# Graph kernel: the sums of two attention layers get more buffers, an earlier load, and a residual that partly moves to TensorE

## The reference, cut to what matters

```python
def gat_conv(x, src, dst, W, a_src, a_dst, b, num_nodes):
    h = jnp.einsum('nd,dhf->nhf', x, W)
    logits = jax.nn.leaky_relu(al_s[src] + al_d[dst], 0.2)
    e = jnp.exp(logits - m[dst])                    # softmax over the edges of a target node
    alpha = e / (z[dst] + 1e-16)
    out = jax.ops.segment_sum(h[src] * alpha[..., None], dst, num_segments=num_nodes)
    return out + b
h   = gat_conv(x, ..., W1, ...)                     # 8 heads
out = gat_conv(h, ..., W2, ...)                     # 1 head
x   = _layernorm(x + out)
```

## Time and profile before

| what | value |
|---|---|
| median of 3 runs | 3779.49 us (3779.07 to 3781.46) |
| the profiled execution's own time | 3806.31 us |
| span of its trace | 3804.5 us |
| busy in the span | PE 3222.5, PEld 2659.1, DVE 2782.3, ACT 1886.4, POOL 2084.1 us |
| softmax of layer 1, by the trace | about 506 to 571.9 us |
| `gat1` | 571.9 to 731.3 us |
| `gather_out1` | 731.3 to 1035.8 us |
| `gat2` | 1035.8 to 1285.45 us |

### The profile page before, as it was taken

One profiled execution on the slowest core, in us unless ns is written; L12 is line 12 of the kernel. 1 busy time (PEld: TensorE's weight loads), 2 busy tenths in 40 slices (PEclk: granted clock), 3 DMA queues, 4 the chain that ended last, 5 costly groups with the idle time before them and its releaser, 6 DMA issues. The chain is left out here.

```text
span 3804.5 us, 56930 instructions
## 1 busy us (share of the span) xinstructions
PE 3222.5 (85%) x15070; PEld 2659.1 (70%) x15070; DVE 2782.3 (73%) x7844; ACT 1886.4 (50%) x5403; POOL 2084.1 (55%) x2118
## 2 busy tenths in 40 slices
PE   5999935588577599856999996999999999999775
PEld 4888824476466366534888885888888787878664
DVE  5666667699688366675677665989989898989742
ACT  3777724466433112134333332666666566666565
POOL 3666600267267566424333333767677676767577
PEclk8999967799799899978999998999999999999997
DMA  4877839644267332247343333878878686868664
GB/s 139 242 242 238 242 106 302 225 128 133 67 197 219 96 89 88 59 145 234 95 125 121 120 119 117 242 210 235 240 212 251 194 252 198 252 200 248 198 218 162
DMA packets 677043, 684.78 MB, mean 180 GB/s; under 512 B 72882, under 2 KB 631015, under 8 KB 676627
## 3 DMA queue, kind: packets, MB, share of 16 engines
q1 hardware_dynamic: 592122, 484.38, 40.8%
q0 software_dynamic: 68160, 181.21, 17.5%
q10 hardware_dynamic: 16444, 15.55, 1.2%
HBM read 401.66 MB, written 283.11 MB: 180 GB/s over the span
## 5 line engine op out<-in xcount | busy, mean ns | idle before, releaser
L2823 PE MATMUL s_i_bank<-s_i_messages,s_i_equal 128*128 128x256 f32 x1200 | 360.5, 383 | 6.9 <-issue 4.4
L622 POOL DMA_INDIRECT s_i_messages<-h,table_row x300 | 305.6, 1019 | 98.0 <-issue 80.8
L932 POOL TENSOR_TENSOR n_powers<-n_powers,neg_half 128x8 f32<-128x8 f32 (+3 forms) x164 | 268.0, 1634 | 165.6 <-issue 59.3
L622 POOL DMA_INDIRECT s_i_messages<-h,table_row_b x300 | 309.2, 1031 | 90.1 <-issue 81.8
L857 ACT ACTIVATE n_z<-gamma_bc,n_powers 128x256 f32<-128x256 f32 x320 | 175.0, 594 | 354.9 <-POOL n_powers L932 354.0
L816 PE MATMUL s_n_bank<-w,n_xt 128*128 128x256 f32 x1280 | 309.1, 385 | 17.8 <-DMA n_xt<-in_x_t 16.8
L834 PE MATMUL s_n_bank<-w_out,n_ht 128*128 128x256 f32 x1280 | 314.0, 390 | 6.5 <-ACT n_ht L844 6.3
L825 PE MATMUL s_n_bank<-n_x3t,w_in 128*128 128x256 f32 x1280 | 303.3, 380 | 0.0
L2852 DVE SCALAR_TENSOR_TENSOR s_i_y<-s_i_bank,s_i_scale,acc 128x256 f32<-128x256 f32 x600 | 285.6, 477 | 5.0 <-remote 5.0
L816 PEld LDWEIGHTS s_n_bank<-w,n_xt 128*128 128x128 f32 x1280 | 246.9, 193 | 53.7 <-DMA n_xt<-in_x_t 17.2
L834 PEld LDWEIGHTS s_n_bank<-w_out,n_ht 128*128 128x128 f32 x1280 | 248.5, 195 | 46.5 <-ACT n_ht L844 11.7
(11 more groups left out here) (452 smaller groups left out, 9268.8 us busy)
## 6 DMA issues: line engine op xcount, KB each, us to landing
h<-s_i_y SPq DMA_DIRECT2D x600, 128.0 KB
n_xt<-in_x_t SPq DMA_DIRECT2D x160, 256.0 KB
out<-n_w SPq DMA_DIRECT2D x160, 256.0 KB
s_i_equal<-eq_tab SPq DMA_DIRECT2D x600, 64.0 KB
x<-s_x_rows SPq DMA_DIRECT2D x100, 256.0 KB
out<-s_a_hs SPq DMA_DIRECT2D x100, 128.0 KB
proj_dst<-s_a_hd SPq DMA_DIRECT2D x100, 128.0 KB
h<-s_h_rows SPq DMA_DIRECT2D x50, 256.0 KB
```

The costliest lines, as they stand in the source:

```text
L622: return net.nc.gpsimd.indirect_dma_start(out, None, table, bass.IndirectOffsetOnAxis(index, 0))
L932: self.nc.gpsimd.tensor_tensor(v[:, 8 + b0:8 + b1], v[:, b0:b1], self.net.neg_half[:, 0:b1 - b0], ALU.pow).then_inc(self.powered, 1)
L2823: nc.tensor.matmul(banks[r % 4][:, 0:D], EQ[q % NM][:], M[q % NM][:], start=True, stop=True).then_inc(summed, 1)
```

## The change

Three places are rewritten.

1. `softmax` of layer 1 now also loads the first seven units of `gat1`: SP issues them behind the load of `src_nodes`. Their buffers (`Feed`, tiles `b_equal` and `b_x`) are allocated around both stages.
2. `gat1` has seven buffers for its loads; unit k's table and features are loaded when unit k - 7 is summed. The keys of the search are the first thing that SP loads in the stage.
3. `gat2` has five buffers for the table and `out1`, six for the gathered `x`, four for `y`, and four PSUM banks for the projection. PE does `total(i)` first in a turn, DVE weighs a unit earlier, POOL issues the gathers ahead of the power. For the first tile of each unit the residual is added by PE: a product of the gathered rows with `spread` (an identity whose row 0 is ones; row 0 of the gathered tile holds the constant `c12`, its gather being sent out of bounds) starts the accumulation. DVE then adds the residual of the second tile alone and takes the first tile's statistics from PSUM, and ACT normalises it from there.

```diff
@@ softmax, SyncE
                 sp.dma_start(net.src_nodes[:], ...).then_inc(nodes_in, 16)
+                for k in range(feed.NB):
+                    feed.load(sp, k)
                 sp.wait_ge(nodes_in, 16)
@@ class Feed: NB = 7
+    def load(self, sp, k):
+        net, b, R = self.net, k % self.NB, self.net.R
...
+        sp.dma_start(self.EQ[b][:], net.eq_tab[tiles, :, :]...).then_inc(self.eq_in[b], 16)
+        sp.dma_start(self.X[b][:, :, 0, :], net.out1[rows, :]...).then_inc(self.x_in[b], 16)
+        sp.dma_start(self.X[b][:, :, 1, :], net.proj_dst[tiles, :, :]...).then_inc(self.x_in[b], 16)
@@ gat1, SyncE
-            for k in range(2):
-                load(k)
             find.load(sp)
-            for k in range(2, N):
-                load(k)
+            for k in range(NB, N):
+                sp.wait_ge(summed, k - NB + 1)
+                sp.wait_ge(msg_ready, k - NB + 1)
+                feed.load(sp, k)
@@ gat2
-    G, NB = 2, 3
+    G, NB, NE, NX = 2, 5, 5, 6
-        Y = st.sb("d_y", [P, G, D], n=3)
+        Y = st.sb("d_y", [P, G, D], n=4)
-        sums, tps, prs = (st.ps(f"d_ps_{n}", 2) for n in ("sums", "t", "p"))
+        sums, tps, prs = (st.ps(f"d_ps_{n}", m) for n, m in (("sums", 2), ("t", 2), ("p", 4)))
@@ gat2, SyncE
-                load(i + 2)
+                load(i + 3)
@@ gat2, GpSimd
+            gp.wait_ge(based, NX + 4)
...
+                get(i + 2)
                 power(i - 3)
-                get(i + 2)
@@ gat2, TensorE, project(k)
                     pe.wait_ge(xt_ready, k + 1)
-                    past(pe, y_ready, k - 1)
+                    pe.wait_ge(x_in[k % NX], ...)
+                    past(pe, x1_ready, k - 3)
                     for g in range(w):
+                        if k < N and g == 0:
+                            nc.tensor.matmul(out, spread[:], X[k % NX][:, g, :], start=True, stop=False)
...
             for i in range(TURNS):
+                total(i)
                 transposes(i - 1)
                 project(i - 2)
-                total(i)
@@ gat2, ScalarE, norm(k)
+                        y = prs[k % 4][0:p, 0:D] if g == 0 else Y[k % 4][:, 1, :]
@@ gat2, VectorE
+            def stats(k):
...
+                    if k < N:
+                        V.tensor_tensor(Y[k % 4][:, 1, :], prs[k % 4][:, D:2 * D], X[k % NX][:, 1, :], ALU.add)
+                    ch(V.bn_stats(s[0:p, 0:6], prs[k % 4][0:p, 0:D]))
+                    if k < N:
+                        ch(V.bn_stats(s[:, 6:12], Y[k % 4][:, 1, :]))
+            for b in range(NX):
+                V.tensor_copy(X[b][0:1, 0, :], net.c12[0:1, :]).then_inc(based, 1)
...
+            weigh(0)
             for i in range(TURNS):
-                weigh(i)
+                weigh(i + 1)
                 aggregate(i - 1)
                 bias(i - 2)
-                join(i - 3)
+                stats(i - 3)
```

More of the change, by code:

```diff
@@ L1274, in _, with softmax @@
                     src.var_1(dve, *v)
-def softmax(net, layer):
+def softmax(net, layer, feed=None):
     nc, T, H = net.nc, net.T, net.H
@@ L1512, in count, with __init__, gat1 @@
             ct.then_inc(self.counted, 1)
-def gat1(net):
+class Feed:
+    NB = 7
+    def __init__(self, net, ctx):
+        nc, self.net, self.G = net.nc, net, 2
+        sb = lambda name, shape: [ctx.enter_context(nc.sbuf_tensor(f"{name}{i}", shape, F32)) for i in range(self.NB)]
+        self.EQ = sb("b_equal", [P, self.G, P])
+        self.X = sb("b_x", [P, self.G, 2, net.D])
+        self.eq_in = [nc.alloc_semaphore(f"b_eq_loaded{i}") for i in range(self.NB)]
+        self.x_in = [nc.alloc_semaphore(f"b_x_loaded{i}") for i in range(self.NB)]
+    def load(self, sp, k):
+        net, b, R = self.net, k % self.NB, self.net.R
+        tiles = slice(k * self.G, (k + 1) * self.G)
+        rows = slice(R + k * self.G * P, R + (k + 1) * self.G * P)
+        sp.dma_start(self.EQ[b][:], net.eq_tab[tiles, :, :].rearrange("g p e -> p g e")).then_inc(self.eq_in[b], 16)
+        sp.dma_start(self.X[b][:, :, 0, :], net.out1[rows, :].rearrange("(g p) d -> p g d", p=P)).then_inc(self.x_in[b], 16)
+        sp.dma_start(self.X[b][:, :, 1, :], net.proj_dst[tiles, :, :].rearrange("g p d -> p g d")).then_inc(self.x_in[b], 16)
+def gat1(net, feed):
     nc, D, T, R, H = net.nc, net.D, net.T, net.R, net.H
-    G, NB = 2, 4
+    G, NB = feed.G, feed.NB
     N = T // G
     with Stage(nc) as st:
-        EQ = st.sb("b_equal", [P, G, P], n=NB)
-        X = st.sb("b_x", [P, G, 2, D], n=NB)
+        EQ, X, eq_in, x_in = feed.EQ, feed.X, feed.eq_in, feed.x_in
         M = st.sb("b_messages", [P, G, 2, D], n=2)
@@ L1531, in gat1 @@
         find = Search(net, st)
-        eq_in, x_in = (st.sem(f"b_{n}", NB) for n in ("eq_loaded", "x_loaded"))
         ends_out, stored = (st.sem(f"b_{n}", m) for n, m in (("ends_stored", 3), ("out1_stored", 3)))
@@ L1892, in store @@
                     sp.wait_ge(x1_ready, k + 1)
-                    sp.dma_start(tiles(net.x1, k), Y[k % 3][:]).then_inc(stored[k % 3], 16)
-            for k in range(2):
+                    sp.dma_start(tiles(net.x1, k), Y[k % 4][:]).then_inc(stored[k % 4], 16)
+            for k in range(3):
                 load(k)
             for i in range(TURNS):
-                load(i + 2)
+                load(i + 3)
                 store_ends(i - 1)
@@ L1908, in get @@
                 if k <= N:
-                    past(gp, y_ready, k - NB + 1)
+                    past(gp, y_ready, k - NX + 1)
                 if k < N:
@@ L1951, in total @@
                         for g in range(G):
-                            mm = nc.tensor.matmul(sums[k % 2][:, g * D:(g + 1) * D], EQ[k % NB][:, g, :], net.out1_src[:, k * G + g, :], start=True, stop=True)
+                            mm = nc.tensor.matmul(sums[k % 2][:, g * D:(g + 1) * D], EQ[k % NE][:, g, :], net.out1_src[:, k * G + g, :], start=True, stop=True)
                         mm.then_inc(summed, 1)
@@ L3010, in build @@
                 project1(net)
-                with nc.sbuf_tensor("src_nodes", [net.T, net.R], I32) as net.src_nodes:
-                    softmax(net, 1)
-                    gat1(net)
+                with nc.sbuf_tensor("src_nodes", [net.T, net.R], I32) as net.src_nodes, ExitStack() as feed_ctx:
+                    feed = Feed(net, feed_ctx)
+                    softmax(net, 1, feed)
+                    gat1(net, feed)
             with nc.sbuf_tensor("scores_2", [P, 2, net.T], F32) as net.scores, nc.sbuf_tensor("out1_src", [P, net.T, net.D], F32) as net.out1_src:
```

82 lines of the change are left out of this document (43 added, 39 removed).

## The result

The changed kernel took 3756.17 us in the median of four runs (3753.27 to 3758.17), the kernel before 3780.47 on the same chip: a ratio of 0.9927 (95% interval 0.9914 to 0.994), 24.3 us or 0.7% faster. The sign was right and the stated range of 3726 to 3757 us held the time, but by 0.8 us, and with luck: the likeliest case's own range ended at 3751, and the rest was there for a rival (late loads) that did not come. The gain is 16 us short of the 40.3 that were forecast. The profiled execution after took 3758.17 us by its own time, with a span of 3756.5.

A forecast was written before the change was run, and what follows sets the result against it. The first sums were taken as bound by transfers, the second sums by a ring of waits with a 4.21 us lap. Terms 4.8 + 5.5 + 30.0 + 0 = 40.3 us off the median 3779.49 gave 3739 us, range 3726 to 3757.

The forecast's parts named there:

- the likeliest case: Whole kernel: all terms together gain 40.3 us, to 3739 us, own range 3730 to 3751; chance 64%.
- late loads: Second sums: a store waiting for lagging POOL holds the next table; turn 3.85, gain 27.9 us, 3752; chance 10%.
- Load in the softmax: Softmax: 4.59 MB of added transfers hide under its work, cost 0; without that cover, 13 us.
- Start of the first sums: Start of gat1: keys issued first land earlier, so everything up to turn 1 starts 4.8 us earlier (3.7 to 5.7).
- Turns of the first sums: gat1 after turn 1: three units' less data left for the DMA-bound stretch, gain 5.5 us (3.5 to 7.5).
- Turns of the second sums: gat2 steady part: 46 turns fall from 4.233 to 3.58 us, gain 30.0 us (25.0 to 32.8).
- The ring: gat2 before the change: aggregate, transposes, projection and sums wait on each other in turn, one lap 4.21 us.
- GpSimd locked out: gat2: gathers wait for DVE's weighing pass (0.47 us), turn about 4.1, gain 16.4 us, 3763; chance 8%.
- The ring stays: gat2: some wait keeps the turn at 4.21; gain 5.9 us, 3774, no change; chance 3%.
- slower: gat2: PE falls from 2.4 to 1.2 GHz, turn 7.04 us; with 20 such turns 3808 us; chance 3%.
- Ramp and tail: Start and end of gat2: aggregates come 3.2 us earlier, the tail gives back 3.3; together 0 (-4 to +3).
- The base: Whole kernel: the 40.3 us are taken off the median before, 3779.49, rather than the profiled 3806.31, giving 3739.

The follow-up runs named there:

- the second trace: The unchanged kernel before, run and traced once more: 3783.42 us, span 3781.6.
- experiment 3: Changed kernel with its seven buffers, but all their loads issued in the first sums' own stage, none in the softmax: ratio 0.9942 to the kernel before.
- the first trace: The kernel before, in the profiled execution that the prediction was made from: 3806.31 us by its own time, span 3804.5.
- Experiments 4: Changed kernel with both gathers of a unit of the second sums without an index bound: ratio 0.987 to the kernel before.
- experiment 6: Changed kernel with bounded gathers kept and the shift product moved from GpSimd to VectorE: ratio 0.9867 to the kernel before.
- experiment 10: Changed kernel with both gathers plain and ScalarE writing the constant into row 0 afterwards: ratio 0.9859 to the kernel before.
- experiment 5: Changed kernel with the x1 stores of the second sums issued from ScalarE's queue: ratio 0.9919 to the kernel before.
- experiment 9: Changed kernel with plain gathers in the second sums, the residual of both tiles on VectorE and no product with spread: ratio 0.9893 to the kernel before.
- experiment 8: Kernel before with an index bound on both gathers of the second sums, all indices inside the table: 3787.12 us in a single run.

## Why the prediction was right, and where not

**Load in the softmax, 0:** right. The softmax took 65.6 us (65.4 and 65.5 before); its DMA share is 0.84 from 540 to 550 us and 0.00 from there to 565, so the loads had ended 15 us ahead of the border.

**Start of the first sums, 4.8:** 4.9 by the second trace (18.0 to 13.1), 5.3 by experiment 3.

**Turns of the first sums, 5.5:** 124.1 to 117.7 is 6.4 us, 5.7 by the first trace (123.4 to the same pass). It is less data left behind turn 1, as forecast: over these 123.4 and 117.7 us both kernels move 341 GB/s, so 1.9 MB less, for the 1.97 MB of three units. The rate didn't rise. The rule with 425 GB/s of the Trainium skill, page "DMA: Bandwidth & Descriptors", section "Where 436 GB/s comes from", would have given 17.6 us; no run here shows that rate.

**Turns of the second sums, 30.0:** the step that failed. It measured 17.0 (46 turns from 4.265 to 3.895; 15.6 by the first trace). The ring is gone, TensorE's turn was 3.46 for a forecast 3.52, VectorE was under it. But "POOL's turn ... 3.69 us" was put together from the gathers of before, and the diff's gathers carry a bound that those don't: the lap is 3.95. The surplus over TensorE is then 0.45 to 0.5 us a turn, some 20 us over the stage, where I let buffers of "about three turns or 10 us" absorb 8. They were used up after a few turns, and from there the turn is GpSimd's. Experiments 4, 6 and 10 show it from three sides, each with a turn of 3.45. My 3.69 was too high as well: for plain gathers it counts a gap of 0.30 behind the product, which is 0.16 in experiment 10, and 0.28 for the product, which is 0.20 there; the lap is 3.46. With them my term would have been 46 x (4.265 - 3.45) = 37 us.

**Rivals.** *Late loads* gave nearly the measured turn and time (3.85 and 3752), for a wrong cause. The sign that I had named for it even came, a turn over 3.8 and VectorE waiting for a table (3.5 us in 120), so that sign could not tell the two apart; experiment 5 did, where the waits for tables were gone and the turn stayed at 3.855. *GpSimd locked out* had a price of that size too (0.47 us a turn); against it, VectorE is busy 108.0 of 120 us in experiment 10, 95.7 in the changed kernel, and the gathers take 0.99 us in the mean there, 1.08 and 1.00 here. So the lock of the Trainium skill, page "SBUF — State Buffer", section "SBUF: two separate sides", is not what lengthened them. A hold of this kind does show, on another instruction: the product of experiment 9, and the 0.28 us product of the earlier trace rows, which ends 0.05 us behind the bias pass in 29 turns of the second trace of before. In the changed kernel the product stands clear of the bias pass and takes 0.20. *The ring stays* and *slower* didn't come; the clock is 1.00 in the steady part. Of the signs of the likeliest case, the turn of 3.5 to 3.7 us and the aggregates without a wait didn't come either.

**Ramp and tail, 0:** held. The fourth aggregate came 15.5 us after the stage's start, where the first trace of before had 19.7 and the second 17.1: 4.2 or 1.6 us gained for a forecast 3.2. From the last aggregate to the next stage it takes 40.0 us, for 35.2 and 36.0: 4.7 or 3.9 lost for 3.3. Together -0.6 or -2.4 us, inside -4 to +3. The sizes agree in part by luck: the sums of unit N started 9.6 us behind that aggregate, where it was 8.1 and 7.9, a term that the forecast had at nothing, and the work behind them took 3.2 or 2.2 us more. The products that queue there, after:

```profile
1219.44 1.15 PE L1970 MATMUL s_d_ps_sums<-s_d_ends,upper 100*100 100x256 f32 x2 [8.50 <-DMA s_d_ends<-ends]
...
1222.08 3.26 PE L2001 MATMUL s_d_ps_p<-w,s_d_xt 128*128 128x256 f32 x8
```

Four products took 3.26 us here, 0.8 each, against 0.47 in mid-stage. The window of 1222.0 to 1225.5 has a mean granted clock of 0.59, and the one ahead of it 0.50, TensorE's lower level of 1.2 GHz, behind 8.50 us in which it stood idle:

```profile
1218.00:1222.00 4.00, 2.56 (x8) 2.16 (x9) 0.76 (x2) 0.53 (x2) 0.00 (x0) 0.50 0.10 39
1222.00:1225.50 3.50, 3.50 (x12) 2.78 (x11) 0.12 (x1) 1.01 (x3) 0.00 (x0) 0.59 0.24 80
```

**The base** was sound: taking the gain from the median and not from the first trace's 3806 kept its 26 us of scatter out.

**Left open:** what GpSimd does in the 0.77 us between a bounded gather's MOVE and its start (experiment 8). That they can overlap earlier work is seen in experiment 6; what they consist of, nothing here shows.

## What to carry to other kernels

When a change gives an instruction one more argument, its price is not that of the instruction in the old trace: ask what the argument adds to the lap of the engine that will be the fullest, and whether buffers really cover the surplus times the number of turns. Behind a change with several parts, look for the engine that waits for nobody; the waits of the others (ends, tables, aggregates) were its consequences. Name signs that tell two rivals apart: a wait for tables belonged to both here. And try the buffers alone before moving work to an engine: here they gave 28.6 us, while the moved residual cost 14.0 until its bound was taken away, and was then worth 9.3.

## What the runs showed of the hardware

A gather with a bound on its indices took 1.00 to 1.08 us where a plain one took 0.95 to 1.02, but it also started 0.5 us later after the wait that let it go (0.80 for 0.28 us), and 0.54 instead of 0.16 us behind a GpSimd product of 0.20; behind the power of 0.81 the gap was 0.19, and behind another gather 0.30 either way. The bounded first gather of a unit starts 0.77 us behind a MOVE of GpSimd that plain gathers don't have (33 of 33 turns of the changed kernel). A GpSimd product of 128x2 that started inside VectorE's bias pass ended 0.05 us behind that pass (39 of 39 turns of experiment 9); gathers that started inside it were not held (6 in experiment 6, 1.06 to 1.10 us). Nor was VectorE held the other way: 42 bias passes that started inside GpSimd's power took 0.41 us in experiment 10. Statistics taken from PSUM cost 0.421 us against 0.407 from SBUF, and the norm from PSUM 0.56 against 0.59, in the changed kernel. Seven units in flight where there were four did not raise the rate of engines that already showed a share of 1.05 (352 GB/s in the earlier trace rows, 354 after); VectorE's waits for features behind the start fell from 16.0 us (24.3 less 8.3 at the start) to 3.7 all the same.
